# Writing out the image loop of all five engines of a fused attention kernel

## The reference, cut to what matters

```python
# block 0: group norm, one-head attention over the 1024 pixels, projection, residual
h = group_norm(x)
q, k, v = split(qkv_w @ h + qkv_b)
x = x + proj_w @ (v @ softmax(q.T @ k * C**-0.5).T) + proj_b
# block 1: t is the image as 1024 tokens of 128; LN, then attention in windows of 32 tokens, 8 heads, and an MLP of 512
t = tokens(x)
t = t + attn_and_mlp(layernorm(t))
# block 2: LN, quantise to fp8 and back, one 128x128 product, residual
t = t + qdq(layernorm(t)) @ qdq(kernel) + bias
```

## Time and profile before

| what | value |
|---|---|
| median of three runs | 2352.03 us |
| the profiled execution | 2352.98 us |
| its span, first to last instruction | 2351.2 us |
| TensorE matmul busy | 2205.4 us, 94% |
| VectorE busy | 1753.6 us, 75% |
| ScalarE busy | 1480.0 us, 63% |
| GpSimd busy | 1229.4 us, 52% |
| mean granted TensorE clock | 0.987 |
| DMA packets of kind "instruction" | 28 on queue q8 (0.46 MB), 18 on q14 (0.15 MB) |

### The profile page before, as it was taken

One profiled execution on the slowest core, in us unless ns is written; L12 is line 12 of the kernel. 1 busy time (PEld: TensorE's weight loads), 2 busy tenths in 40 slices (PEclk: granted clock), 3 DMA queues, 4 the chain that ended last, 5 costly groups with the idle time before them and its releaser, 6 DMA issues.

```text
span 2351.2 us, 62343 instructions
## 1 busy us (share of the span) xinstructions
PE 2205.4 (94%) x21902; PEld 1605.7 (68%) x21902; DVE 1753.6 (75%) x5668; ACT 1480.0 (63%) x2881; POOL 1229.4 (52%) x1323
## 2 busy tenths in 40 slices
PE   4999999999999999999999999999999999999984
PEld 3677766677776677776677776677777677767663
DVE  5677777777787777787777787777787787787753
ACT  2566666766666766666666666666666666666653
POOL 5255554555554555554555555555555555555544
PEclk8999999999999999999999999999999999999997
DMA  1111111111111111111111111111111111111110
GB/s 44 35 31 33 42 36 45 38 33 29 44 36 45 38 33 30 42 36 45 41 31 33 39 36 45 42 29 35 36 36 45 44 28 36 35 36 45 36 28 19
DMA packets 76094, 86.08 MB, mean 37 GB/s; under 512 B 20624, under 2 KB 55440, under 8 KB 76048
## 3 DMA queue, kind: packets, MB, share of 16 engines
q1 hardware_dynamic: 62368, 52.44, 9.3%
q10 hardware_dynamic: 13680, 33.04, 4.3%
HBM read 18.29 MB, written 16.78 MB: 15 GB/s over the span
## 4 chain that ended last, share of the span: by engine, by line
PE 72%; DVE 10%; ACT 8%; issue 4%; DMA 3%; SPq 3%; POOL 1%; ACTq 0%; DVEq 0%; POOLq 0%
PE ps L976 15%; PE ps L1072 10%; PE ps L870 9%; PE ps L872 9%; PE ps L871 9%; PE ps L957 4%; PE ps L1040 4%; ACT y L493 3%; PE ps L1022 3%; PE ps L934 2%; PE ps L988 2%; DMA ptbd<-et 2%; PE ps L923 1%; SPq L330 1%; SPq L323 1%
## 5 line engine op out<-in xcount | busy, mean ns | idle before, releaser
L380 POOL TENSOR_TENSOR rstd<-veps,halfpow 128x4 f32<-128x4 f32 x256 | 264.5, 1033 | 531.6 <-DVE veps L750 531.6
L976 PEld LDWEIGHTS ps<-vg,p 128*128 128x128 f32 x4096 | 505.6, 192 | 40.4 <-ACT p L524 6.5
L976 PE MATMUL ps<-vg,p 128*128 128x129 f32 x4096 | 523.2, 277 | 0.9 <-ACT p L524 0.9
L524 ACT ACTIVATE p<-ps 128x512 f32<-128x512 f32 x512 | 291.9, 589 | 128.1 <-PE ps L872 104.3
L705 DVE TENSOR_REDUCE cm<-ps 128x1 f32<-128x512 f32 x512 | 334.7, 680 | 16.2 <-PE ps L934 16.1
L414 POOL TENSOR_TENSOR e<-e,srec 128x512 f32<-128x512 f32 x128 | 134.3, 1049 | 243.2 <-DVE srec L793 240.2
L1072 PE MATMUL ps<-w,hid 128*128 128x128 f32 x2048 | 241.7, 276 | 1.7 <-ACT hid L576 1.7
L1072 PEld LDWEIGHTS ps<-w,hid 128*128 128x128 f32 x2048 | 236.2, 192 | 7.6 <-issue 1.8
L576 ACT ACTIVATE hid<-ps,cols 128x512 f32<-128x512 f32 x256 | 165.8, 684 | 97.7 <-PE ps L872 97.7
L934 PE MATMUL ps<-kgh,qgh 128*128 128x512 f16 x512 | 176.0, 384 | 40.6 <-DVE qgl L699 34.1
L957 PE MATMUL ps<-shift,minus 128*128 128x512 bf16 x512 | 194.5, 380 | 2.0
(11 more groups left out here) (184 smaller groups left out, 5508.6 us busy)
## 6 DMA issues: line engine op xcount, KB each, us to landing
ptbd<-et SPq DMA_DIRECT2D x512, 64.0 KB, 2.1
kbd<-kk SPq DMA_DIRECT2D x512, 32.0 KB, 2.0
out_y<-o_sb ACTq DMA_DIRECT2D x64, 256.0 KB, 2.4
x_sb<-in_x ACTq DMA_DIRECT2D x31, 512.0 KB, 3.9
x_sb<-in_x SPq DMA_DIRECT2D x1, 512.0 KB, 3.4
e<-in_w_t SPq DMA_DIRECT2D x1, 256.0 KB, 3.7
w<-in_w_t SPq DMA_DIRECT2D x1, 256.0 KB, 3.7
hid<-in_in_w_t SPq DMA_DIRECT2D x1, 192.0 KB, 2.4
```

The source lines that it names most:

```text
L380: g.tensor_tensor(rstd[:, k, h, :], veps[:, k, h, :], halfpow[:], ALU.pow).then_inc(s[f"ln_pow{k}"], 1)
L524: sc.activation(p32[:, c % PRING, :], bank("st", c), ACT.Exp, scale=C ** -0.5).then_inc(s["p_made"], 1)
L976: last = mm(ps[:, b, at:at + PVW], p32[:, c % PRING, part], vg32[:, j, :], start=j == 0 and q % 2 == 0, stop=j == MT - 1, skip_group_check ...
```

## The change

The body of the loop is no longer run by a hardware loop. For every engine in `WRITTEN_OUT`, which are all five, the 28 rounds are written out one after the other. The function `iteration` is called with the same kind ("steady"), so the steps, their order and the PSUM banks stay the same; only the image number is now a Python integer. With it the register instructions and the branches go, the waits' values and the DMA addresses become constants, and the program's text is as long as the work: 32 images' worth for each engine, where there were the written-out passes and one body.

```diff
@@ -90,6 +90,7 @@
 BANK = {(name, index): b for name, index, _, b in ORDER["pe"] if b is not None}
+WRITTEN_OUT = ("pe", "dve", "act", "pool", "sp")
 PROLOGUE = ("load_x", "gn0", "gn1", "gn2")
@@ -282,8 +283,12 @@
             for i in ahead:
                 iteration(i, i)
-            with engine.Fori(loop.start, loop.stop) as i:
-                iteration("steady", i)
+            if key in WRITTEN_OUT:
+                for i in loop:
+                    iteration("steady", i)
+            else:
+                with engine.Fori(loop.start, loop.stop) as i:
+                    iteration("steady", i)
             for i in after:
                 iteration(i, i)
```

## The result

The changed kernel takes 2375.1 us (median of four runs, 2365.00 to 2383.64) beside 2352.62 us (four runs) before: a ratio of 1.011, 95% interval 1.007 to 1.015. It is 22.5 us slower, where 18 were forecast. Its profiled execution is the quickest of the four, 2365.0 us with a span of 2363.3 us. All sizes from its trace are those of that execution, which is 12 us slower than the profiled one of before and not 22.

The account below looks back on a forecast made before the run. It took TensorE, busy 68 of 70.5 us a pass, as the bound. A net 18 us, between 14.7 by period and 25 by hit, gave 2353 + 18 = 2371 us profiled, 2370 on the median; range 2347 to 2392 us.

Parts of the forecast that it names:

- Part one: At the turn of each pass, branches, register instructions and computed waits go: a gain of 28 x 0.05 = 1.4 us.
- the gain of part one stays: Rival, 3%: at TensorE's transposes of `y`, 0.48 us stay an image, 28 x 0.48 = 13.4 us faster, 2339 us.
- Part two: Code brought in, 154 large and 98 small packets, delays SyncE's DMAs within SBUF, for which TensorE waits: 2.1 hits an image.
- Way (a): Price by period: three periods before the loop are 0.59 us longer in the mean, 28 x 0.59 = 16.6 us, 14.7 net.
- hits are swallowed: Rival, 20%: every pass behaves as the first written-out one, +0.04 us, so no change, 2351 us.
- much slower: Rival, 13%: every hit passes at the size of TensorE's wait, mean 0.76 us: 45 us less 1.9, 2395 us.
- (b): Price by hit: 0.46 us a hit, 28 x 2.1 x 0.46 = 27 us, 25 net of the loop's own fetches.
- (4): Sign: new TensorE waits for `kbd` and `ptbd`, 15 to 40 us in all, with SyncE issues of 1.4 us by the dozen.
- (3): Sign: TensorE's wait for `qgl` near 0.6 us an image, about 20 us in all; that for `y` grows about as much.
- (6): Sign: the same clock and the same matmul busy time as in the kernel before.
- (5): Sign: marks of the passes no longer evenly 70.42 us apart, but between 70.4 and 72, mean about 71.1.
- The rule: Trainium skill: taken branches outside the two-page window stall, straight code mostly hides page crossings, so full unrolling would be a gain.

Follow-up runs that it names:

- all_but_tensor: The changed kernel with TensorE's loop kept and the other four engines written out: 2338.22 us, ratio 0.994 to the kernel before.
- only_vector: The changed kernel with only VectorE's loop written out, the other engines looped: 2348.77 us, ratio 0.998 to the kernel before.
- only_scalar: The changed kernel with only ScalarE's loop written out, the other engines looped: 2341.1 us, ratio 0.994 to the kernel before.
- no_placing_tensor: The changed kernel without SyncE's placing DMAs (output not the reference's), TensorE alone written out: 2335.67 us, 1.5 us from the all-looped kernel without placing.
- only_tensor: The changed kernel with only TensorE's loop written out, the other four looped: 2390.09 us, ratio 1.016 to the kernel before.
- tensor_two_a_round: The changed kernel with all engines looped, but TensorE's body holding two passes, 14 rounds instead of 28: 2435.15 us, ratio 1.037 to the kernel before.
- no_placing_looped: The changed kernel with all engines looped and SyncE's 1024 placing DMAs left out (output not the reference's): 2334.13 us beside 2346.18 for the kernel before.
- scalar_and_vector: The changed kernel with ScalarE and VectorE written out, TensorE, GpSimd and SyncE looped: 2335.1 us, ratio 0.993 to the kernel before.
- moved_by_half_a_block: The changed kernel with 64 tiny float32 matmuls added in TensorE's prologue, meant to move its later code half a packet, in fact 256 instructions: 2388.89 us.

## Why the prediction was right, and where it was not

**The bound and the form of passes.** That written-out passes of the old trace are the change's passes was the right source. Marks 70.46, 70.74 and 71.84 us apart have their like in a list that now runs from 69.94 to 74.65.

**Part one, mis-sized tenfold.** The step "both waits together are 1.36 us looped and 1.31 us written out: 0.05 us stays" stopped at the second wait of the pass. Behind it the wait for `kk` (0.23 us) goes as well and that for the other `y` falls (0.19 to 0.11), and 0.48 us stay a pass: 28 x 0.48 = 13.4 us, which `all_but_tensor` measures as 14.7. My reason for the step was wrong too: I priced VectorE's 0.48 us, the largest figure at the turn, and put ScalarE's 0.14 aside. `only_vector` gives 4 us and `only_scalar` 12. The rival "the gain of part one stays" had the right amount, but named the wrong wait as the place where it decides. In the written-out pass that I compared, the gain was there and hidden: a hit had used it up (0.53 us of wait at 168.50). I read its 70.46 us as a pass in which little was gained and little lost; by the undisturbed pass of 69.94 us and that wait (their sum is 70.47) it was one with a gain of 0.5 and a loss of 0.5.

**Part two, right in mechanism.** Packets: 177 and 106 for some 175 and over 100. Hits: 55 in the 31 periods, 1.8 each, for 2.1 (six more lie behind the last mark; 34% of the packets for 39%). The cause, placing DMAs with hardly any slack, is shown by `no_placing_tensor`. Its price was low: 0.46 us a hit forecast, 0.63 measured. The mean was drawn from passes some of which held the hidden gain; and the sum had no term for the clock, which some 3 us of the profiled run go to. Way (a), 0.59 us a period, was the sounder, since gain and loss are both in it: `only_tensor`'s 37 less 14.7 are 22.5 us, or 0.8 a pass.

**The sum.** 18 us forecast, 22.5 measured. Both terms were too small, by 13 and by 18 us, on opposite sides, so the good total is partly luck. The rival "hits are swallowed" fails by the placing waits; "much slower" (45 us gross) is nearer to `only_tensor`'s 37 than my own (b) was, and only the gain hid it.

**The signs to look for.** (1), (2) and (4) came as said: the waits for `kbd` and `ptbd` are 35.9 us. (3) holds for `qgl`; the wait for `y` grew less than that fell, by 5.7 us for 11.6. (6) holds for the means (clock 0.987, matmuls busy 2207.7 us for 2205.4) and hides the two places where the clock fell. (5) holds in kind, though the marks lie 69.94 to 74.65 us apart and not 70.4 to 72: the 28 periods from the fourth mark to the last average 71.08 us in the profiled run, where about 71.1 was said, and the other three runs, of which there is no trace, are 9 to 19 us longer. Their mean granted clock is 0.983 to 0.984 for the profiled one's 0.987, which fits with more such falls but doesn't show them.

**The rule.** For this kernel's loop it did not bear, and the forecast rightly went by the rows. `tensor_two_a_round` shows when it does. Crossing packets in straight code is indeed nearly hidden for the engine whose code it is (0.08 us a pass in `no_placing_tensor`); the price is paid here in waits for the placing DMAs.

## What to carry to other kernels

Writing out a loop is a choice for each engine: it pays where register work sits in a hand-over that the pass hangs on (ScalarE here, 12 us from 0.1 us each), and costs where the body is large and was resident (TensorE, 37 us). Count the code packets that a form needs, and ask what small DMAs with little slack they will meet. When two forms of one pass stand in a trace, compare undisturbed passes to the last wait, not to the first one that evens out.

## What the runs showed of the hardware

A packet of 16 KB of code lasts 0.9 to 1.6 us in the change (1.0 in the median), and a DMA issue of SyncE that it meets takes up to 1.7 us for 0.6. A placing DMA whose landing falls together with a load of `x` and a packet took up to 5.7 us, where 4.2 was the longest before, with a load of `x` alone. From the line of the placed probabilities in the changed kernel:

```profile
DMA to landing us min/median/max: 2.0/2.1/5.7
```

The prologue comes in two lengths. The time from the first mark to the second was 52 to 53 us in the profiled runs of the change, `tensor_two_a_round`, `no_placing_looped`, `no_placing_tensor` and `scalar_and_vector`, and 59 to 60 us in those of before and the others, but for `moved_by_half_a_block`. It seems to vary from run to run and not with the kernel: of the 17 runs of before beside `only_tensor` two took 2343.6 and 2344.0 us, and fifteen 2351.2 to 2356.6. In before, TensorE waits 11.4 us for `cparts` there, in the change 2.8. What decides between them was not tried. It would explain some 6 us of scatter between runs, and why the change's profiled run is only 12 us behind that of before: from the fourth mark to the last the change is 16.3 us longer, and 5.4 us are given back ahead of it.
